# Three convolutions and a mixture of experts on one core: from 16-row strips with 11 matmuls a chunk to two interleaved column halves, with 3 full matmuls and 12 on 64x64 tiles of the array

## The reference

```python
x = x + conv3x3(_gn(x), L0_conv_weight, L0_conv_bias)     # x: (4, 8, 256, 256)
x = x + conv3x3(_gn(x), L1_conv_weight, L1_conv_bias)
x = x + experts(_gn(x), L2_conv_w1, L2_conv_b1, L2_conv_w2, L2_conv_b2)
x = x + conv3x3(_gn(x), L3_conv_weight, L3_conv_bias)
...
def experts(x, w1, b1, w2, b2):        # one expert for each of the 8 channels
    h = gelu(einsum('bend,edf->benf', x, w1) + b1)         # 256 -> 1024
    return einsum('benf,efd->bend', h, w2) + b2            # 1024 -> 256
```

## Time and profile before

| what | value |
|---|---|
| median of 3 runs | 646.5 us (645.26 to 646.52) |
| the profiled execution | 645.57 us, of which its span is 643.8 us |
| PE busy | 608.4 us, 94% of the span, 2937 matmul records |
| DVE, ACT, POOL busy | 392.3, 324.4 and 149.4 us |
| mean granted clock of TensorE | 0.994 |

### The profile page before, as it was taken

The page is one execution under the profiler, slowest core; times in us unless marked ns, Lnnn a source line. Parts: engine busy times, 40 slices in busy tenths (PEclk is TensorE's granted clock), DMA queues, the critical chain, the costliest instruction groups (busy, mean ns, idle before and its releaser), DMA issues.

```text
span 643.8 us, 9687 instructions
## 1 busy us (share of the span) xinstructions
PE 608.4 (94%) x2937; PEld 294.4 (46%) x2937; DVE 392.3 (61%) x683; ACT 324.4 (50%) x444; POOL 149.4 (23%) x188
## 2 busy tenths in 40 slices
PE   1888999999999899999999999999999999799987
PEld 1534444445545444444444444444444455455433
DVE  6885878867778564908529166192570669767222
ACT  0687645589766753516336154352452464737510
POOL 4567555663221100000000000000010102645420
PEclk9999999999999999999999999999999999989999
DMA  8141111101303103011101111011200000123353
GB/s 345 66 162 52 42 46 48 46 13 36 103 10 132 65 1 130 2 66 65 65 11 54 65 65 65 0 65 65 65 0 0 0 2 1 47 80 116 160 193 114
DMA packets 6451, 42.84 MB, mean 67 GB/s; under 512 B 1002, under 2 KB 1082, under 8 KB 3482
## 3 DMA queue, kind: packets, MB, share of 16 engines
q1 hardware_dynamic: 6272, 42.47, 18.5%
q10 hardware_dynamic: 154, 0.05, 0.0%
HBM read 25.21 MB, written 8.39 MB: 52 GB/s over the span
## 4 chain that ended last, share of the span: by engine, by line
PE 74%; POOL 5%; DVE 5%; DMA 5%; ACT 4%; issue 4%; POOLq 0%; SPq 0%; ACTq 0%; DVEq 0%
PE PS L1107 24%; PE PS L1130 23%; PE PS L1017 19%; PE PS L1030 5%; POOL XN L435 3%; DMA HALO<-XN 3%; ACT XN L514 2%; PE PS L1071 2%; DVE ST L684 1%; DMA BB<-L_conv_b 1%; DMA X<-x 1%; ACT SCR L508 1%; POOL RS L417 1%; DVE HID L897 1%; DVE X L792 1%
## 5 line engine op out<-in xcount | busy, mean ns | idle before, releaser
L1017 PE MATMUL PS<-XN,CWT 128*128 128x512 f16 (+1 forms) x864 | 202.7, 381 | 2.3 <-ACT XN L514 1.0
L1130 PE MATMUL PS<-HID,W2S 128*128 128x512 f16 x768 | 170.0, 379 | 0.0
L1107 PE MATMUL PS<-XT,W1S 128*128 (+1 forms) x768 | 168.8, 379 | 0.2 <-DVE XT L784 0.2
L1017 PEld LDWEIGHTS PS<-XN,CWT 128*128 128x128 f16 x864 | 84.4, 100 | 98.6 <-issue 4.3
L435 POOL TENSOR_TENSOR XN<-SCR,XN 128x512 f32 (+1 forms) x96 | 110.7, 1157 | 66.7 <-ACT XN L514 64.0
L556 ACT ACTIVATE SCR<-PS,BT 128x512 f32<-128x512 f32 x128 | 86.9, 686 | 65.8 <-DVE HID L897 36.2
L1107 PEld LDWEIGHTS PS<-XT,W1S 128*128 128x128 f16 x768 | 75.1, 98 | 89.0 <-issue 0.7
L1130 PEld LDWEIGHTS PS<-HID,W2S 128*128 128x128 f16 x768 | 75.1, 98 | 86.8 <-issue 0.3
L508 ACT ACTIVATE SCR<-X,SC 128x512 f32 (+1 forms) x96 | 77.5, 807 | 73.7 <-POOL SC L424 39.1
L758 DVE SCALAR_TENSOR_TENSOR X<-PS,X 128x512 f32<-128x512 f32 (+1 forms) x96 | 65.4, 687 | 75.4 <-PE PS L1030 75.3
L897 DVE SCALAR_TENSOR_TENSOR HID<-SCR,HID 128x512 f16<-128x512 f32 x128 | 88.5, 691 | 13.6 <-ACT HID L582 9.5
(11 more groups left out here) (63 smaller groups left out, 262.4 us busy)
## 6 DMA issues: line engine op xcount, KB each, us to landing
W1F<-L_conv_w SPq DMA_DIRECT2D x8, 1024.0 KB, 4.8
W2F<-L_conv_w SPq DMA_DIRECT2D x8, 1024.0 KB, 4.8
HALO<-XN SPq DMA_DIRECT2D x44, 181.3 KB
X<-x SPq DMA_DIRECT2D x3, 2048.0 KB, 12.3
out<-X SPq DMA_DIRECT2D x3, 2048.0 KB, 7.0
out<-X SPq DMA_DIRECT2D x8, 256.0 KB, 2.0
X<-x SPq DMA_DIRECT2D x1, 1536.0 KB, 7.0
X<-x SPq DMA_DIRECT2D x1, 512.0 KB, 7.7
```

The costliest lines, as they stand in the source:

```text
L1017: pe.matmul(bank(k), CWT[:, l, w, kx], rhs, start=(n == 0), stop=False)
L1107: mm = pe.matmul(bank(ft % RING), W1S[:, w, h * NF + ft * P:h * NF + (ft + 1) * P], XT[:, p, h, :, e, part], start=(n == 0), stop=(n == 3 ...
L1130: mm = pe.matmul(bank(G2_BANK + h), W2S[:, w, ft * NW + h * P:ft * NW + (h + 1) * P], HID[p][:, part, ft], start=(ft == 0 and part == 0 an ...
```

## The change

Almost the whole program is written anew. The parts that matter:

- The 128 partitions now are 2 column halves times 8 channels times 8 rows: even columns of the image on partitions 0 to 63, odd ones on 64 to 127 (`W2`, `R = 8`). A strip is 8 rows by 128 columns, an image 32 strips; a chunk is again 512 columns, now four strips. A full matmul then reaches both halves: one shift of the columns (`centre`, 3 matmuls for the three products) covers the middle tap and one neighbour of each half. The missing neighbour of each half comes from the other half, shifted by one: two 64x64 matmuls for each product (`sides`). The rows above and below come from HALO, again one 64x64 matmul for each half and product (`halo`, with 48 rows and one of ones).
- `tiles` issues the sides of a chunk together with the halo of the chunk before it, 4 by 4, so that the four tiles of a round have different quarters of the array.
- HALO has twice the size; its copies go in two halves of an image with 8 copies each. The tiles of chunk 1 are the first that wait for the first half.
- ACT and POOL work on pieces of two chunks (1024 columns); PSUM banks in turn are 5 in place of 4.
- The weight bands are laid out by the host and loaded; before, POOL and DVE built them. `PRE` chunks are made by POOL in place of ACT. Image 2 is transposed during the first hidden layer, in place of during step 7.
- Halo, pads and statistics are placed anew: statistic 14's variance is at the first pair of step 9, statistic 15's at the first pair of step 10.

```diff
-        def conv_main(g, i, k):
...
-            for part, w in ((0, 0), (0, 1), (1, 0)):
...
-                for kx in range(KX):
-                    rhs = XN[s][:, part, ds(i * TC, TC), kx:kx + NW]
-                    pe.matmul(bank(k), CWT[:, l, w, kx], rhs, start=(n == 0), stop=False)
...
-            for w in range(2):
-                rhs = HALO[s][0:KH, ds(i * TC, TC), 0:NW]
-                mm = pe.matmul(bank(k), CWT[0:KH, l, w, 3], rhs, start=False, stop=(w == 1))
...
+        def centre(g, i):
...
+            for n, (part, w) in enumerate(((0, 0), (0, 1), (1, 0))):
+                if n == 0:
+                    pe.wait_ge(hi_ok, PIECE_OF[g, i] + 1)
+                if n == 2:
+                    pe.wait_ge(lo_ok, PIECE_OF[g, i] + 1)
+                pe.matmul(to, CWT[:, w, l, 0:P], XN[s][:, part, rows, 1:NJ + 1],
+                          start=(n == 0), stop=False)
+
+        def sides(g, i, part, w, last):
...
+            odd = pe.matmul(bank(k, HALF_P, P), CWT[0:HALF_P, w, l, SIDE:EDGE],
+                            XN[s][0:HALF_P, part, rows, 2:NJ + 2], start=False, stop=False)
+            even = pe.matmul(bank(k, 0, HALF_P), CWT[HALF_P:P, w, l, SIDE:EDGE],
+                             XN[s][HALF_P:P, part, rows, 0:NJ], start=False, stop=False)
...
+        def halo(g, i, part, w, last):
...
+            even = pe.matmul(bank(k, 0, HALF_P), CWT[0:kh, w, l, EDGE:CWN],
+                             HALO[s][0:kh, part, rows, 0:NJ], start=False, stop=last)
+            odd = pe.matmul(bank(k, HALF_P, P), CWT[HALF_P:HALF_P + kh, w, l, EDGE:CWN],
+                            HALO[s][HALF_P:HALF_P + kh, part, rows, 0:NJ],
+                            start=False, stop=last)
...
+        def tiles(chunk, behind):
...
+                arrived = halo_a if i < SPLIT else halo_b
+                pe.wait_ge(arrived[g % 2], HALO_HALF * (g // 2 + 1))
...
+            for n, (part, w) in enumerate(PRODUCTS):
+                if chunk is not None:
+                    sides(*chunk, part, w, n == 2)
+                if behind is not None:
+                    halo(*behind, part, w, n == 2)
...
+            sp.wait_ge(lo_ok, PIECE_OF[g, SPLIT] + 1)
+            halo_part(s, 0, NT // 2, halo_a[s])
+            sp.wait_ge(lo_ok, PIECE_OF[g, NCH - 1] + 1)
+            halo_part(s, NT // 2, NT, halo_b[s])
...
+        def slot_free(g):
+            act.wait_ge(norm_ok, stat_of_step(g) + 1)
+            if g >= 2:
+                act.wait_ge(side_mm, 2 * NCH * (g - 1))
+                act.wait_ge(halo_a[g % 2], HALO_HALF * (g // 2))
+                act.wait_ge(halo_b[g % 2], HALO_HALF * (g // 2))
...
+        for g in range(8, 12):
             before_step(g)
-            conv_chunks(g, 0, RING)
-            conv_chunks(g, RING, NCH)
+            for k in range(NPR):
+                q = NCH * g + 2 * k
+                centre(g, 2 * k)
+                tiles((g, 2 * k), ((q - 1) // NCH, (q - 1) % NCH) if q > 8 * NCH else None)
+                centre(g, 2 * k + 1)
+                if (g, k) == (8, 0):
+                    group_mean(13)
+                if (g, k) == (8, 1):
+                    group_variance(13)
+                if g < 10:
+                    result_transposes(g - 6, 2 * k)
+                    result_transposes(g - 6, 2 * k + 1)
+                tiles((g, 2 * k + 1), (g, 2 * k))
+                if g < 10 and k == NPR - 1:
+                    group_mean(g + 6)
+                if 8 < g < 11 and k == 0:
+                    group_variance(g + 5)
```

More of the change, by code:

```diff
@@ L97, in image_of_step, with bass_program @@
     return g % 4
[L100 to L112, removed]
+def bass_program(nc, x, consts, cw, w1, w2, out):
     ctx = ExitStack()
@@ L216, in bass_program, with pre, xt_part @@
[L216 to L219, removed]
+    def pre(m):
+        return PRE[:, m % NCH] if m < 3 * NCH else PRE3[:, m % NCH]
+    def xt_part(m, part):
+        b, j = m // NCH, m % NCH
+        tt = (b % 2) * NT + j * TC
+        return XT[:, b // 2, tt:tt + TC, :, :, part, :].rearrange("p t h c r -> p (t h c) r")
+    def tr_bank(m):
+        return bank(TR_BANK + m % 2).rearrange("p (k r) -> p k r", r=R)
@@ L230, in bass_program @@
+    zero_ok = [sem(f"zero_ok{s}") for s in range(2)]
+    cw_hi, cw_ok = sem("cw_hi"), sem("cw_ok")
     bn_ok = sem("bn_ok")
-    mv_in = sem("mv_in")
     mv_ok = sem("mv_ok")
@@ new lines, in low_parts, with pre_chunk @@
+        def low_parts(g):
+            for k in range(len(pieces(g))):
+                low_part(FIRST_PIECE[g] + k)
+        def pre_chunk(m):
+            b, j = m // NCH, m % NCH
+            if m == 0:
+                pool.wait_ge(cw_ok, 1)
+            if NCH <= m < 3 * NCH:
+                pool.wait_ge(pre_mm, m - NCH + 1)
+            if m == 3 * NCH:
+                pool.wait_ge(conv_mm, 2 * NCH * 8)
+            pool.wait_ge(norm_ok, 8 + b + 1)
+            pool.tensor_scalar(pre(m), x_chunk(b, j), SC[:, 8 + b, 0:1], SC[:, 8 + b, 1:2],
+                               ALU.mult, ALU.add).then_inc(pre_ok, 1)
@@ L481, in _ @@
+        zero_halo(1, 1)
+        zero_pads(1, 1)
+        for k in range(2, len(pieces(8))):
+            low_part(FIRST_PIECE[8] + k)
+        for g in range(9, 12):
+            scale_and_bias(g + 4)
+            low_parts(g)
     @block.scalar
     def _(act):
-        act.wait_ge(wk_zero, 1)
-        act.dma_start(WK[0:WROWS - 1], cw.rearrange("c x l y o -> (c x) l y o")
-                      ).then_inc(cw_in, 16)
-        act.dma_start(WK[WROWS - 1:WROWS, :, 0], cb.unsqueeze(0)).then_inc(cw_in, 16)
@@ new lines, in slot_free, with normalise @@
+        def slot_free(g):
[4 more added lines that the diff above has]
+                act.wait_ge(halo_b[g % 2], HALO_HALF * (g // 2))
+            if g == 8:
+                act.wait_ge(hid_ok, NE * NPAIR * FT)
+            if g in (8, 9):
+                act.wait_ge(g2_mm, 4 * (NE - 1) + 2 * (g - 7))
+        def normalise(g):
+            slot_free(g)
+            for k in range(len(pieces(g))):
+                normalise_piece(FIRST_PIECE[g] + k)
@@ L669, in _ @@
         last_hidden(e)
-        normalise(8, 0, 1)
+        slot_free(8)
+        normalise_piece(FIRST_PIECE[8])
         result(e, 1, 0)
-        normalise(8, 1, 2)
+        normalise_piece(FIRST_PIECE[8] + 1)
         result(e, 1, 1)
-        normalise(8, 2)
+        for k in range(2, len(pieces(8))):
+            normalise_piece(FIRST_PIECE[8] + k)
         for g in range(9, 12):
@@ L858, in _ @@
+        dve.scalar_tensor_tensor(out=CWT[:, 1].rearrange("p l k -> p (l k)"),
+                                 in0=CWF[:].rearrange("p l k -> p (l k)"), scalar=WS,
+                                 in1=CWT[:, 0].rearrange("p l k -> p (l k)"),
+                                 op0=ALU.mult, op1=ALU.subtract).then_inc(cw_ok, 1)
+        for i in range(NCH):
+            input_stats(0, i)
+        aggregate(0)
         deviation(0)
-        build_product(0, 1)
         variance(0)
-        build_product(0, 2)
@@ L1147, in expert @@
                     output(e, p, h)
[L1150 to L1160 removed]
+        pe.wait_ge(cst_in, 16)
         group_mean(0)
@@ L1164, in _ @@
         for _ in range(WARM_UP):
[L1165 to L1166 removed]
+            pe.matmul(PS[:, 0:P], GRP, IDF, start=True, stop=True)
+        for g in range(8):
             before_step(g)
[L1169 to L1180 removed]
```

1063 lines of the change are left out of this document (452 added, 611 removed), and 3 rows, old and new, of the table STAT_AT.

## The result

| kernel | median, us | ratio to before (95% interval) |
|---|---|---|
| before | 645.9 (644.9 to 646.5, 4 runs) | |
| changed | 674.3 (672.5 to 675.2, 4 runs) | 1.044 (1.041 to 1.047) |

A forecast was written before the change was run, and what follows sets the result against it. PE was taken to bound the kernel, never lacking work within a step. From 643.8, less 17.4 (first stage), plus 1.6 (MLP) and 6.5 (third convolution), comes 634.5; with 1.8 and 0.9 added, 637 us; range 606 to 678.

The forecast's parts named there:

- Four tiles at a time: PE, side and halo tiles: four quarters of the array work together, 12 tiles in 3 rounds of 0.216 us.
- chunk pitch: PE, convolution steps: time per chunk, forecast 1.75 us (14.0 a step), where it was 2.39 before.
- change-over: PE, between full matmuls and tiles: the array may have to empty, 0.22 us each, two a chunk.
- so I take 2.6, between 2 and 5.3: Halo copies of each step: landing after the last issue taken as 2.6 us, from rows of 3.49 and 5.26.
- N to the last low part: From a step's normalisation start N through ACT and POOL: three pieces done at N + 8.9 us, four at N + 11.
- issues of 4.5 us: SP, first half image's halo copies: seven issues at 0.64 us are 4.5, then 0.6 for the last.
- slow copies: Rival, halo copies: they land 3 us later than taken on nine steps of the path, 664 us; chance 0.13.
- two quarters at a time: Rival, PE tiles: two quarters cannot write one bank together, rounds 0.43, chunk 2.4 us, total 670; chance 0.20.
- forecast's own range: Whole kernel: 622 to 652 us, for 1.5 to 2.0 us a chunk, POOL's 1.5 to 2.3, two restarts more or less.
- second pair of images: MLP: with image 2's transposes in the first hidden layer, it opens after 29.5 us in place of 27.9.
- restart: PE after a wait for halos: the clock's restart costs 3.0 us, charged in the sum.
- Third convolution: Last stage: statistics 13 to 15 stand behind halo tiles; T + 109.5 in place of T + 103, 6.5 us lost.

The follow-up runs named there:

- spread-rows kernel: Changed kernel with halo copies writing every third or sixth HALO partition in place of 16 or 8 neighbouring ones, edge weights permuted to match: 633.7 us, ratio 0.980.
- best version: Changed kernel with spread halo rows, plus statistics 13 to 15 and statistic 1 put ahead of the tiles that wait for a halo: 611.0 us, ratio 0.946.

## Why the prediction was wrong

**The array: right.** Four tiles at a time, rounds of 0.22. The chunk pitch was forecast at 1.75 and is 1.54; with 6 x 0.216 for the matmuls, 0.12 a change-over fits in place of 0.22.

**The step that failed: "so I take 2.6, between 2 and 5.3".** The mechanism around it was right (SP's eight issues, then the landing, then PE, on nine steps), and so were N to the last low part and the issues of 4.5 us. The landing after the last issue was 7.2 us, outside its own bounds. They came from copies of 24 rows of larger packets and took for granted that a landing depends on bytes. It is 4.6 us too little, 4.3 with small gains beside it, and on nine steps that makes 38 of the 38.8 us. That the two numbers agree so closely is in part luck, since the smaller errors below cancel. The prediction had this case as a rival, slow copies, at 664 with 3 us a step and a chance of 0.13; mechanism and steps were right there, but its size came from the same rows and was too small. The 674.3 us lie within the stated range of 606 to 678 mainly because of the rival with two quarters at a time (670), whose mechanism did not occur; the forecast's own range ended at 652, and it said faster.

The spread-rows kernel tests this by correcting it: there the landing is 2.95, near the 2.6, and the steps come within 2.6 us of where the prediction put them (first ACT row, us; MLP is the first MLP matmul, T the start of the third convolution):

| | N(0) | N(1) | N(3) | N(5) | MLP | T | N(9) | N(10) | N(11) | end |
|---|---|---|---|---|---|---|---|---|---|---|
| forecast | 15.9 | 45.2 | 82.1 | 113.3 | 182 | 525 | 557.4 | 578.5 | 598.7 | 634.5 |
| spread rows | 17.4 | 46.4 | 80.2 | 112.4 | 179.4 | 526.3 | 558.0 | 578.6 | 598.9 | 631.9 |
| changed | 17.4 | 49.9 | 88.7 | 123.1 | 202.3 | 549.1 | 584.8 | 609.7 | 634.6 | 673.3 |

**Smaller errors.** The changed and the spread-rows kernel open the second pair of images 33.5 us after the first MLP matmul (forecast 29.5): the chain has there, after 217.89 in the changed kernel, two small POOL operations of 2.53 and 0.77 us for statistic 11 and a `PRE` chunk of 1.15, which the prediction did not put on the path. With spread rows, an MLP that starts 2.6 us sooner than forecast and the shorter pitch make up for it.

**The clock: right in size, wrong in worth.** The 3.0 us that the sum charges for a restart are what the 8 and 9 matmuls of the earlier trace rows lose: they take 3.59 and 3.30 us (granted clock 0.50 and 0.60 there), where 8 x 0.216 + 0.163 = 1.89 and the 1.95 of the earlier trace rows for nine are full clock. A restart in the changed kernel is 2.75 us, but filling the waits gave 3.9 us once and nothing on the best version. The prediction counted each restart in full on the path; where one was avoided altogether (steps 9 and 11 with spread rows), 0.9 and 1.3 us arrived.

**Third convolution: right in its direction.** It was forecast to lose 6.5 us although each chunk is cheaper, since statistics stand behind the halo. It loses 21, with four landings of 4.3 us too much in it; with its statistics moved it falls from 124.2 to 108.7 us, with spread rows alone to 105.6, with both to 97.0, where before it took 103.0.

## What to carry to other kernels

When a change moves data into more and smaller SBUF-to-SBUF copies, ask for each copy which partitions it writes, not only how many bytes (landings of 7.2 and 2.95 us here for the same bytes): permuting rows cost nothing here, where the weights were permuted with them (633.7 us in place of 674.3, with the same packets and bytes). A bound for a transfer taken from copies of another shape is no bound (5.26 us from the copies before, 7.2 measured). And once the array is made cheaper, look for each small operation (here a statistic of one column) that stands in its queue behind a new wait.

## What the runs showed of the hardware

- Copies of the same bytes in the same packets land 7.2 us after the last issue when they write 16 and 8 neighbouring partitions, and 2.95 when they write every 3rd and 6th; the engine time of the queue falls from 220 to 162 us.
- Two 64x64 tiles with different rows of the array write one PSUM bank at once (different partitions), rounds 0.22 us apart, and weights for four tiles are loaded within that time (0.10 to 0.11 us each, side by side).
- Where PE had idled for 2.88 us behind matmuls at full clock, the next rounds were 0.43 apart, half clock (granted 0.50); after 2.96 us the first two rounds were still at full clock (granted 1.00) and the third was not (0.50); after 1.47 and 1.91 us all were (1.00). In the kernel before, the matmuls of the earlier trace rows at a granted clock of 0.50 came behind 3.14 us in which PE idled.
- A DVE operation of one column took 1.95 us in place of 0.22 when a POOL operation of 2.06 us had begun 0.12 us before it, and both ended within 0.01 us.
